# Attention and expert kernel on one core: the open-mask flag asked three steps earlier, list constants moved, the wait for constants moved, fourteen unread passes left out

## The reference, cut to what matters

```
x = x + xattn(layernorm(x), ctx, ctx, mask_BxS2, mask_BxSxS2)   # 8 batches of 256 x 256, 16 heads of 16
x = x + ffn(layernorm(x))                                       # 8 experts 256 -> 1024 -> 256, top 2 of 8

q, k, v = layernorm(x) @ Wq.T, ctx @ Wk.T, ctx @ Wv.T
attn = where(mask, q @ k.T / sqrt(16), -inf);  p = softmax(attn)
xattn = (p @ v) @ Wo.T + bo
gate = softmax(y @ w_gate.T);  ffn = sum over the top 2 of gate * (gelu(y @ W1 + b1) @ W2 + b2)
```

## Time and profile before

| | us |
|---|---|
| timed runs, median (lowest to highest) | 503.3 (500.13 to 503.98) |
| profiled execution, its own time | 498.93 |
| its span | 497.7 |
| PE busy in the span | 446.9 (90%) |
| DVE, ACT, POOL busy | 360.7, 324.1, 178.0 |

### The profile page before, as it was taken

How to read it: one execution, slowest core, us unless ns; L and a number is a source line. 1 busy time by engine, 2 the same in 40 slices (tenths; PEclk the granted TensorE clock), 3 DMA queues, 4 the chain that set the end, 5 groups by cost and what they waited for, 6 DMA issues and landing times.

```text
span 497.7 us, 10201 instructions
## 1 busy us (share of the span) xinstructions
PE 446.9 (90%) x3599; PEld 372.9 (75%) x3599; DVE 360.7 (72%) x784; ACT 324.1 (65%) x521; POOL 178.0 (36%) x220
## 2 busy tenths in 40 slices
PE   4897989999998986958889989999999999999992
PEld 3464657766775763637889989999898898998982
DVE  3166776877777784446978998698788787987871
ACT  1131777766766643445969876898778878878860
POOL 6043431433601268720372515245321223212323
PEclk9999999999999997766999999999999999999997
DMA  6657533253222012368376899897797988888822
GB/s 231 191 137 239 195 115 117 107 165 110 94 90 86 25 66 83 127 232 313 115 239 200 270 285 253 242 265 256 228 266 220 282 255 262 277 259 234 286 37 34
DMA packets 44624, 93.19 MB, mean 187 GB/s; under 512 B 6990, under 2 KB 30350, under 8 KB 38684
## 3 DMA queue, kind: packets, MB, share of 16 engines
q1 hardware_dynamic: 35340, 81.56, 50.1%
q0 software_dynamic: 7152, 9.46, 9.5%
q10 hardware_dynamic: 2080, 1.49, 1.0%
HBM read 63.10 MB, written 14.32 MB: 156 GB/s over the span
## 4 chain that ended last, share of the span: by engine, by line
PE 61%; DVE 8%; issue 8%; POOL 8%; DMA 6%; ACT 5%; SPq 2%; ACTq 1%; DVEq 0%; POOLq 0%
PE bank L1376 15%; PE S L1340 11%; PE bank L1443 5%; PE S L1353 4%; PE S L1475 4%; PE bank L1510 4%; DVE nmax L935 3%; POOL x2n L607 3%; PE bank L1418 2%; PE bank L1426 2%; PE S L1498 2%; PE bank L1435 2%; DMA lists<-zero 2%; PE S L1548 2%; POOL lists L617 2%
## 5 line engine op out<-in xcount | busy, mean ns | idle before, releaser
L576 POOL DMA_INDIRECT out<-y,slot x39 | 73.0, 1873 | 161.4 <-DVE y L844 78.3
L935 DVE TENSOR_REDUCE nmax<-S 128x4 f32<-128x1024 f32 x64 | 78.3, 1223 | 43.3 <-PE S L1475 40.6
L1340 PE MATMUL S<-xgT,Q 128*128 128x256 f32 x512 | 97.1, 289 | 2.7 <-DVE xgT L812 2.6
L1250 ACT ACTIVATE prob<-S 128x1024 f32<-128x1024 f32 x64 | 65.7, 1026 | 26.0 <-PE S L1498 25.0
L1340 PEld LDWEIGHTS S<-xgT,Q 128*128 128x128 f32 x512 | 79.9, 192 | 3.2 <-issue 2.1
L789 DVE TENSOR_TENSOR K<-w_in,Q 128x1024 fp32r<-128x1024 f32 x46 | 56.4, 1226 | 24.2 <-ACT Q L1116 24.0
L1340 PE MATMUL S<-xgT,K 128*128 128x256 f32 x256 | 72.7, 284 | 0.0
L1154 ACT ACTIVATE hf<-S,b1c 128x256 f32<-128x256 f32 x128 | 53.1, 467 | 29.4 <-PE S L1340 28.8
L1376 PE MATMUL bank<-W2p,hp 128*128 128x256 f32 x528 | 67.9, 285 | 0.0
L1376 PEld LDWEIGHTS bank<-W2p,hp 128*128 128x128 f32 x528 | 64.6, 191 | 0.0
L1116 ACT ACTIVATE Q<-w_in 128x1024 fp32r<-128x1024 f32 x46 | 48.2, 1049 | 13.2 <-DMA w_in<-in_W 13.2
(11 more groups left out here) (205 smaller groups left out, 814.3 us busy)
## 6 DMA issues: line engine op xcount, KB each, us to landing
w_in<-in_W SPq DMA_DIRECT2D x46, 1024.0 KB, 7.1
K<-flat_k SPq DMA_DIRECT2D x24, 256.0 KB, 2.4
Q<-flat_q SPq DMA_DIRECT2D x24, 256.0 KB
xg<-lists SPq DMA_DIRECT2D x16, 265.0 KB, 5.5
b_in<-in_b SPq DMA_DIRECT2D x23, 128.0 KB, 6.2
lists<-zero SPq DMA_DIRECT2D x9, 265.0 KB, 9.2
cin<-in_ctxT SPq DMA_DIRECT2D x8, 256.0 KB, 3.3
xin<-in_x SPq DMA_DIRECT2D x8, 256.0 KB, 3.9
```

Source lines behind the costliest of these rows:

```text
L576: st_y[i % 4].after(pool.indirect_dma_start(out=out, out_offset=bass.IndirectOffsetOnAxis(ap=slot[i % 4][:, t:t + 1], axis=0), in_=y[i % 2 ...
L935: max_done.after(dve.tensor_reduce(nmax[n % 4][:, :, :, m].rearrange("p t r -> p r t"), S1[:].rearrange("p r (t k) -> p r t k", t=TT), AX. ...
L1250: exp_done.after(act.activation(prob[s % 4][:].rearrange("p r t l -> p (r t l)"), S2[:].rearrange("p r l -> p (r l)"), ACT.Exp, scale=SCALE))
L1340: ins = pe.matmul(h_bank[pair][:, u, 0:n], W1p[k][a][:, kc, m * P:(m + 1) * P], xgT[k][c][:, kc, 0:n], start=(j == 0), stop=(j == len(term ...
```

## The change

Four edits. The 38 list fills on GpSimd (now list_constants) move from ahead of the steps to step 2 of GpSimd's stream. VectorE's wait for pool_const moves from the head of its stream into all_open, ahead of the wait for the flag's product. FLAG goes from -4 to -7, so that the flag's product stands directly behind Q's product of batch 0 in TensorE's stream, ahead of the unread passes of step -6, and all_open stands at the top of step -7 in VectorE's stream, ahead of Q's low part. The unread passes go from 12 to 10 at step -6 and from 12 to none at step 0.

```diff
--- before.py
+++ after.py
@@ -628,17 +628,21 @@
                 pool.wait_ge(c_hi.sem, n - IN_TERMS + 1)
                 c_lo.after(pool.tensor_tensor(cT[1][:], cin[n % 2][:], cT[0][:].bitcast(F32), ALU.subtract))
 
-            pool_r.after(pool.memset(taken[:], 0.0))
-            for k in range(CHUNKS):
-                pool_r.after(pool.memset(bounds[:, k:k + 1], float(TS * (k + 1))))
-            for k in range(WHOLE):
-                pool_r.after(pool.memset(number[:, k:k + 1], float(k)))
-                pool_r.after(pool.memset(halves_[:, k:k + 1], float(TS * k + P + 1)))
-                pool_r.after(pool.memset(halves_[:, WHOLE + k:WHOLE + k + 1], float(TS * k + 1)))
-            for i in range(2):
-                pool_r.after(pool.memset(rise[i][:, NE - 1:NE], float(NE * REGION)))
+            def list_constants():
+                pool_r.after(pool.memset(taken[:], 0.0))
+                for k in range(CHUNKS):
+                    pool_r.after(pool.memset(bounds[:, k:k + 1], float(TS * (k + 1))))
+                for k in range(WHOLE):
+                    pool_r.after(pool.memset(number[:, k:k + 1], float(k)))
+                    pool_r.after(pool.memset(halves_[:, k:k + 1], float(TS * k + P + 1)))
+                    pool_r.after(pool.memset(halves_[:, WHOLE + k:WHOLE + k + 1], float(TS * k + 1)))
+                for i in range(2):
+                    pool_r.after(pool.memset(rise[i][:, NE - 1:NE], float(NE * REGION)))
+
             for s in range(START, LAST):
                 now = due[s]
+                if s == 2:
+                    list_constants()
                 if s in (5, 6):
                     weight_low("kq"[s - 5])
                 if "c_lo" in now:
@@ -884,6 +888,7 @@
 
             def all_open():
                 ps, done, full, _ = bank_of("flag", 0)
+                dve.wait_ge(pool_const.sem, POOL_CONSTS)
                 dve.wait_ge(pe_misc.sem, full)
                 flag_any.after(dve.tensor_scalar(any_mask[:], ps[:, 0:1], float(P), None, ALU.is_ge))
                 done.after(dve.tensor_copy(identb[:], ident[:]))
@@ -1037,7 +1042,6 @@
                 rows_done.after(dve.tensor_reduce(rows[i % 2][:, 1, 0:nt], off[1][:, 0:nt], AX.X, ALU.max))
 
             working = iter(())
-            dve.wait_ge(pool_const.sem, POOL_CONSTS)
             for s in range(START, LAST):
                 now = due[s]
                 if 0 <= s < NP:
@@ -1630,9 +1634,9 @@
                 if s >= UNIT_STEP:
                     pe_unit(s - UNIT_STEP)
 
-        FLAG = -4
+        FLAG = -7
         UNITS_IN_STEPS = LAST - UNIT_STEP
-        UNREAD = {-6: 12, 0: 12}
+        UNREAD = {-6: 10}
         POOL_CONSTS = pool_constants()
         pe_attention(range(START, 0))
         pe.wait_ge(flag_any.sem, 1)
```

## The result

The changed kernel took 500.66 us in the median of 12 runs (497.42 to 504.12), the kernel before 503.56 in 12 runs beside them (500.13 to 508.43). The ratio is 0.9939, with a 95% interval of 0.9911 to 0.9966. The profiled execution took 497.42; on another chip the same kernel showed no gain (the ninth experiment).

A forecast was written before the change was run, and what follows sets the result against it. TensorE was taken to bound the kernel (61% of the chain), with a strictly serial opening. Of 1.35 + 2.76 + 0.6 + 1.2 = 5.9 us removed, 3.4 arrive: 503.3 - 3.4 = 499.9 us, range 496.2 to 503.8.

The forecast's parts named there:

- the sum: Whole kernel: first scores 3.4 us earlier, all of it reaching the end, 499.9 us against the median; chance 0.55.
- Statistics and fills: Opening: only both moves together bring the inverse deviation from 8.32 to about 7.0 and turning 1.2 us earlier.
- Flag, load, branch: Opening: flag asked at 14.4, not 19.08; load and branch, 1.35 us, hidden under the passes or behind them, left undecided.
- What is late next: Ahead of the first scores: Q's stacked copies land at 20.0 and release the scores at 20.05, TensorE idle about 1.7 us.
- the tightest follower: Batch 1's statistics in VectorE's stream, after the first scores: just make it at 21.7; a slip costs 0.5 us at most.
- The length of Q's product: Opening, TensorE: the stretch from turning to the end of Q's product keeps its 5.61 us, ending at 14.4.
- The clock in the new idle time: Rival after TensorE's idle ahead of the first scores: clock falls, costing 1 to 3 us, 501.9; chance 0.20.
- The rival that ends slower: From first scores to 43.0: clock stays low through the steps, 15.6 us lost, 515.5; chance 0.05.
- More than the sum: Low-clock stretches around 190 to 217: earlier start makes one fall less, giving 3 us back, 496.5; chance 0.10.
- Arrival at the end: After the opening: the 3.4 us reach the end; the rival, lost between 185 and 217, gives 503.3, chance 0.10.
- Theory B: Experiments' rival on the opening: the passes left out alone make the change's whole gain, ratio 0.994; no chance given.

The follow-up runs named there:

- e9: The changed kernel itself run again without any edit, as a control on another chip, against the kernel before; ratio 1.0011.
- e5: VectorE's wait for constants moved from its stream head, list fills left ahead of GpSimd's steps, flag and passes as before, against the kernel before; ratio 0.9975.
- e2: Only the flag moved to step -7, passes kept at 12 and 12, against the kernel before; ratio 0.9954.
- e3: Only the passes changed, to 10 at step -6 and none at step 0, against the kernel before; ratio 0.9983.
- e6: The changed kernel without its ten passes at step -6; ratio to the kernel before 1.0012.
- e7: The changed kernel with the loads of Wv and the output bias issued later, at step 3; ratio to the kernel before 0.9901.
- e8: The changed kernel with six passes put back at step 0; ratio to the kernel before 0.9933.
- e12: Flag and passes of the change, without its moves of the statistics' wait and the list fills; ratio to the kernel before 1.0017.
- e10: The changed kernel with the loads of Wv and the output bias at step 3 and twelve passes at step 0; ratio to the kernel before 0.9944.
- e4: The changed kernel with the twelve passes of step 0 put back; ratio to the kernel before 0.9878.
- e1: Only the list fills and the statistics' wait moved, flag and passes as before, against the kernel before; ratio 0.9949.
- e11: The changed kernel with the loads of Wv and the output bias at step 3 and eight passes at step 0; ratio to the kernel before 0.9949.

## Why the prediction was right, point by point

**The measured time** is inside the range, and the gain of 2.9 us is near the 3.4 of the sum, but it is made of other parts than the sum. On another chip the same kernel gained nothing (e9), so that the number was met so closely is in part luck.

**Statistics and fills: right.** Forecast 5.65, 7.0 and 8.75 for statistics, inverse deviation and turning; measured 5.58, 7.09 and 8.73. That moving the wait alone does not move the inverse deviation or the turning is what e5 shows; moving the fills alone was not run.

**Flag, load, branch: right.** The hidden branch, left open in the prediction, is shown by e2. Their 1.35 us are off the path. One small thing was missed: with Q's product at the high clock the flag's column open_ is ready last, and TensorE idled 0.34 for it ahead of the ten passes. It cost nothing, since the copies came later still.

**What is late next: right.** Q's copies release the first scores: named by the profile in e3 and e6, and moved by moving other transfers (e7). From the first copy's issue to the scores I took about 5.0 (16.23 to 21.2); it measured 17.89 - 12.83 = 5.06. The statistics of batch 1, the tightest follower, just made it here (19.57, 1.68 behind the scores as before) and slipped by 0.16 and 0.34 in e8 and e9, inside the 0.5 allowed.

**The length of Q's product: not foreseen.** I kept the 5.61 from turning to its end. In the first profile after it was 12.17 - 8.73 = 3.44, since the clock had risen right behind K's product: 1.8 of the 2.2 lie in Q's product and 0.4 in the turning. That moved the first scores to 17.89 and not 20.05. It does not come with the change in every execution: e9, the changed kernel, has 3.43 for Q's product, and e3, whose statistics are those of before, has 1.97. Yet the change may help it. Of the nine profiles with the early turning six have 1.96 or 1.97, of the five with the turning at 9.96 only e3. In three of these five (e2, e5, e12) the clock had risen by 8.0 and fell again at 11.0 to 11.4, with TensorE idle for 1.59 to 1.83 ahead of the turning; in e10, where it rose at 7.8 and the idle time was 0.47, it stayed high. No run separates this from luck, so some 2.2 us of the -5.61 at step 0 hang on the execution.

**The clock in the new idle time: the rival came true, in the mechanism and in the upper end of its price.** I took the idle time at 1.7 and put it on the safe side of the rows. That was a misreading: they give the clock over the idle stretch itself, and by that measure the 3.0 us of the profile after are safe too (1.00 in the window 14.90 to 17.90), though the clock fell 1.2 behind them. The stretch of 1.8 that ends at 193.5 was followed by a fall at 195.1, with a second idle time of 1.11 between. The idle time ahead of the first scores was 3.0 to 3.7 in e3, e9, e12 and the profile after, and the clock fell right behind it in all four. It was at most 2.03 in e2, e4, e7 and e8, and the clock held in all four. The first maxima were 5.61 ahead and 2.68 two steps later: a price of 2.9 against 1 to 3 forecast; in e9 it was 3.94 - 2.92 = 1.0. The step that failed is the time at which the passes end: 18.3 forecast, 14.9 and 16.0 measured in the two profiles of the changed kernel. From 14.4 to 18.3 I gave the ten passes 3.9; wholly at the high clock they took 2.32 in both. The copies meanwhile move with Q's product. Passes that run at high clock end early and leave more idle time. The rule of the Trainium skill that the prediction quoted (TensorE: Matmul & The Clock Gate, "HAM oscillation"), that idle waits between bursts bring the slow clock back, is what these runs show; I gave it too little weight.

The length of an idle time alone does not settle it: in 8 of the 14 profiles (e1, e3, e5, e6, e7, e9, e11, e12) the clock also fell at 43 to 49, at an idle time of 0.5 that follows one of 1.3, and both stand in the same place where it held. That cost 1.2 us between the maxima of steps 2 and 24 (53.0 to 53.1 us apart without this fall, 54.15 to 54.31 with it), and 2.4 in e7, where the clock was low twice as long (55.5). The rival that ends slower, low clock up to 43, did not occur: it was low for 3.4 to 6.8 us here. That the three passes of each step and the products ended it is likely and was not tested. In *More than the sum*, 499.9 less 3 is 496.9 and not 496.5; nothing hangs on it.

**Arrival at the end: mostly right on the first chip, open on another.** The lead was constant from step 2 to step 60. Then 1.2 us were lost. e2 helps to see how: its lead was the same 2.70 at step 24, and it kept 2.69 through step 63, with the clock high until 185.2. In the changed kernel the clock fell at 176.2, and its lead was gone at step 63. All 14 profiles fit that the fall did it: from the maximum of step 61 to that of step 62 it took 5.40 us in the nine in which the clock fell there (after, e1, e3 to e6, e9, e11, e12), and 2.96 or 2.97 in the five in which it did not. TensorE's idle time there is 1.29 in the profile after and 1.27 in e2, so what decides about the fall is open. By the last exponential 2.08 of the lead was back, since the kernel before had its own fall at 188.3. Behind step 63 transfers of weights and the clock move the end by more than the change does. In e2 the gelu that starts at 467.14 before started at 465.54, 1.60 ahead, and the next pair at 470.04, 0.54 behind (469.50). Between them stands this wait for a load of weights in e2's chain, which the chain of before does not have there (start, us, what):

```profile
460.34 8.71 DMA w_in<-in_W
```

Then the clock was low from 475.3 to 482.2, where before it was high, and the span ended 3.0 later than before (500.7). So a single profile cannot weigh 3 us in this kernel, and twelve runs on one chip do it barely.

**Theory B**, that the passes left out are the gain, is refuted twice: alone they show nothing (e3, whose interval leaves out theory B's 0.994), and with twelve put back the gain is still there (e4: 0.9878, with an interval that ends at 0.9942), where theory B asked for 0.999. On that chip the statistics and the flag have each a gain of their own (e1, e2), the passes none.

## A version that is faster

e4 is the fastest on its chip at 0.9878 (from five runs), and e7 at 0.9901 on another. Both together (e10) are 0.7% under the changed kernel on the third. So I would keep the twelve passes of step 0 and load Wv and the bias later; whether both are needed is not settled.

## What to carry to other kernels

When waits are taken off an opening, look for the transfer that ends last behind them, and read how long the tensor engine will idle for it: dense work without a reader that lay wholly inside that wait cost nothing here and kept the clock (e4), so it should be sized by the wait and not cut with it. Where two things hold the same release (a wait, and other work ahead of the releaser), taking one away moves nothing, as e5 showed. And a gain of 0.6% needs its control on every chip on which it is claimed.

## What the runs showed of the hardware

- The load of the flag and the branch cost no time on TensorE with 12 passes queued ahead of them (e2). With the passes ended they cost 1.35 us in the chain of before and 1.38 in that of e1.
- Eight fp32 products of 128x256 take 1.97 to 1.99 us at the high clock and 3.75 to 3.78 at the low one. Whether the clock rises during K's first product or right behind it differs from execution to execution of the same kernel: it did in the profile after (high from 8.9), not in e9 (13.4).
- The clock can fall behind short idle times, and the same ones do not always bring a fall: 1.3 and 0.5 us ahead of 43 to 49 did in 8 of 14 profiles.
- Three copies of 256 KB took 5.0 to 5.3 us from first issue to their reader beside 384 KB of loads (seven experiments and the profile after), and 3.83 and 3.86 without them (e7, e11).
- Two chips' runs were 2 to 3% longer than a third's, with the same kernel (medians of the kernel before). Between the two profiles of the changed kernel the difference stood behind step 60: 1.0 us there, 15.4 at the last exponential, 15.0 at the end.
